# A macaron transformer layer on one core: the projection's stacked parts turned by f32r products with an identity, and one group's softmax maxima made in attention instead of the projection

## What is computed

```
x = x + 0.5 * ffn(layernorm(x))       # 8 experts of width 256, the 2 best of each row
x = x + attention(layernorm(x))       # 16 query heads, 4 key/value heads, head size 32
x = x + 0.5 * ffn(layernorm(x))

# attention
q, k, v = x @ wq, x @ wk, x @ wv      # 512, 128 and 128 columns
q, k = rope(q), rope(k)
p = softmax(causal(q k^T / sqrt(32)))
out = (p v) @ wo
```

## Time and profile before

| what | value |
|---|---|
| median of 3 runs | 1275.9 us (1274.03 to 1278.19) |
| the profiled execution's own time | 1275.88 us |
| its span in the trace | 1274.6 us |
| busy: PE, DVE, ACT, POOL | 93%, 71%, 52%, 47% of the span |
| projection, from the first product to the last copy | 273.5 to some 413.6 us |
| attention, first score to the last four | 413.96 to 1002.31 us |

### The profile page before, as it was taken

One profiled execution on the slowest core, in us unless ns is written; L12 is line 12 of the kernel. 1 busy time (PEld: TensorE's weight loads), 2 busy tenths in 40 slices (PEclk: granted clock), 3 DMA queues, 4 the chain that ended last, 5 costly groups with the idle time before them and its releaser, 6 DMA issues.

```text
span 1274.6 us, 20931 instructions
## 1 busy us (share of the span) xinstructions
PE 1179.8 (93%) x6837; PEld 757.3 (59%) x6837; DVE 910.2 (71%) x2132; ACT 659.6 (52%) x1305; POOL 600.5 (47%) x496
## 2 busy tenths in 40 slices
PE   4899999989998999999999999999999879999996
PEld 3678888758776544444545455445443346777774
DVE  8767777779997776576678787688755675666664
ACT  2545555536455554355456566356567744444442
POOL 4945444313210111001437556556582554888886
PEclk9899999999999999999999999999999999999999
DMA  9923333556530032013445845556633453666665
GB/s 335 367 96 108 111 109 108 174 168 120 96 63 4 34 70 35 1 53 83 99 101 159 173 100 125 174 133 173 135 93 66 139 204 66 100 102 102 101 105 73
DMA packets 68552, 148.44 MB, mean 116 GB/s; under 512 B 8832, under 2 KB 29312, under 8 KB 64448
## 3 DMA queue, kind: packets, MB, share of 16 engines
q0 software_dynamic: 35184, 93.34, 34.4%
q1 hardware_dynamic: 33264, 53.77, 12.4%
HBM read 81.28 MB, written 33.55 MB: 90 GB/s over the span
## 4 chain that ended last, share of the span: by engine, by line
PE 55%; DVE 19%; DMA 9%; issue 8%; POOL 6%; ACT 4%; SPq 0%; DVEq 0%; ACTq 0%; POOLq 0%
PE bank L839 10%; PE bank L1633 8%; PE bank L1645 8%; PE bank L997 7%; PE bank L862 5%; PE bank L1680 5%; DVE PM L1010 4%; PE bank L1663 3%; DVE bank L1012 3%; DMA out<-Y,DI 3%; POOL out L789 3%; DMA CD<-P 2%; DMA XG<-xn,TK 2%; PE bank L821 2%; PE bank L1395 2%
## 5 line engine op out<-in xcount | busy, mean ns | idle before, releaser
L1728 ACT ACTIVATE P<-bank 128x512 f32<-128x512 f32 (+3 forms) x640 | 304.6, 534 | 253.9 <-PE bank L1633 244.4
L1010 DVE TENSOR_REDUCE PM<-bank 128x1 f32<-128x512 f32 x384 | 252.4, 683 | 66.1 <-PE bank L997 65.7
L997 PE MATMUL bank<-Ks,Qs 96*128 96x512 f32 (+3 forms) x640 | 234.9, 387 | 15.1 <-DVE PM L1012 7.8
L1633 PE MATMUL bank<-Qs,Ks 98*128 98x512 f32 (+3 forms) x640 | 241.9, 408 | 5.7 <-ACT P L1728 3.4
L1633 PEld LDWEIGHTS bank<-Qs,Ks 98*128 98x128 f32 x640 | 116.6, 189 | 141.4 <-ACT P L1728 73.5
L1784 POOL TENSOR_SCALAR_AFFINE_SELECT P<-P 128x512 f32<-128x512 f32 x64 | 44.2, 702 | 277.3 <-ACT P L1728 228.8
L997 PEld LDWEIGHTS bank<-Ks,Qs 96*128 96x128 f32 x640 | 121.3, 190 | 64.3 <-DVE PM L1010 22.7
L1645 PE MATMUL bank<-P,V 128*32 128x512 f32 (+3 forms) x1280 | 152.0, 547 | 4.3 <-POOL P L1784 4.3
L1012 DVE CUSTOM_DVE_ANT_0 bank<-bank,KB 128x128 f32<-128x128 f32 (+3 forms) x256 | 124.1, 495 | 40.2 <-PE bank L997 39.6
L789 POOL DMA_INDIRECT out<-Y,DI x78 | 128.1, 1643 | 38.5 <-issue 32.6
L1798 POOL TENSOR_TENSOR CH<-CH,P 128x512 f32<-128x512 f32 x108 | 139.4, 1442 | 14.0 <-ACT P L1728 13.4
(11 more groups left out here) (193 smaller groups left out, 1935.9 us busy)
## 6 DMA issues: line engine op xcount, KB each, us to landing
CD<-P POOLq DMA_DIRECT2D x17, 1024.0 KB, 7.3
xn<-XN SPq DMA_DIRECT2D x8, 1024.0 KB, 7.9
WR<-L_ffn_w POOLq DMA_DIRECT2D x16, 512.0 KB, 15.6
XO<-y POOLq DMA_DIRECT2D x8, 1024.0 KB, 9.4
WR<-L_ffn_w SPq DMA_DIRECT2D x16, 512.0 KB, 7.8
CD<-P SPq DMA_DIRECT2D x7, 1024.0 KB, 5.3
CD<-CH POOLq DMA_DIRECT2D x7, 1024.0 KB, 6.8
XA<-y POOLq DMA_DIRECT2D x24, 256.0 KB, 4.2
```

Source lines behind the costliest of these rows:

```text
L997: pe.matmul(bk(g, bank)[:, 0:n], g.Qs[b][0:96, G % 4 * 4 + h, c * P:c * P + P], g.Ks[0:96, G % 4, k * BQ:k * BQ + n], start=True, stop=Tru ...
L1010: dve.tensor_reduce(dst, bk(g, bank)[:, 0:n], AX.X, ALU.max).then_inc(s(f"free{bank}"), 1)
L1633: pe.matmul(bk(g, bank)[:, o:BQ], g.Ks[0:98, G % 4, k * P:k * P + P], g.Qs[G // 4][0:98, G % 4 * 4 + j, o:BQ], start=True, stop=True).then ...
L1728: act.activation(a.P4[buffer_of(n)][:, j, o:BQ], bk(g, score_bank(g, i))[:, o:BQ], ACT.Exp, scale=scale).then_inc(s("exp"), 1)
```

## The change

Three edits. First, `stack` makes its 20 pieces with ordinary f32r products: `p.N` is the stationary operand as before and a copy of the identity in f32r, `p.IR`, the moving one. ACT makes that copy once at the start of the projection. Before, they were f32 transposes. Second, with EARLY = 3 only groups 0 to 2 have their tops in the projection (48, five in each odd tile from 5, six in each even one, the last four in tile 13, none in 14 and 15); group 3's 16 tops and its solvemax open attention's list. Third, the factor of the spread in attention is 1.13 in place of 1.1.

```diff
@@ memory
+    p.IR = t("IR", [P, P], F32R)
@@ project_plan
-    ahead = [key for G in range(4) for key in tops_of(G)]
+    ahead = [key for G in range(EARLY) for key in tops_of(G)]
...
-                if (total - done) % (total // 8) == 0 and done > total // 4 and i > 4 and ahead:
+                if (total - done) % (total // 8) == 0 and done > total // 4 + total // 8 * (i % 2) and i > 4 and ahead:
...
-        if told < (64 - len(ahead)) // 16:
+        if told < (16 * EARLY - len(ahead)) // 16:
@@ act_project
+    act.copy(p.IR[:], g.ident)
@@ pe_project, stack
-                ins = pe.transpose(bk(g, bank)[0:96, h * P:h * P + P], Nf[:, 4 * q + h, :], ident)
+                ins = pe.matmul(bk(g, bank)[0:96, h * P:h * P + P], p.N[:, 4 * q + h, :], p.IR[:], start=True, stop=True)
@@ attend_plan
-    ahead = [key for G in range(4, 4 * NB) for key in tops_of(G)]
+    ahead = [key for G in range(EARLY, 4 * NB) for key in tops_of(G)]
...
-            while ahead and given < 1.1 * weight:
+            while ahead and given < 1.13 * weight:
```

More of the change, by code:

```diff
@@ L19 @@
 KT = 4 * NB
+EARLY = 3
 F32 = mybir.dt.float32
@@ L1128, in project_plan @@
             told += 1
-    assert told == 4
-    g.shared = [("found", G) for G in range(4)]
+    assert told == EARLY
+    g.shared = [("found", G) for G in range(EARLY)]
 def turned_from_n(g, i):
@@ L1359, in pe_project @@
     s, pe, p, ident = g.s, g.nc.tensor, g.p, g.ident
-    Nf = p.N[:].bitcast(F32)
     def transp(i):
@@ L1507, in attend_plan @@
     ring, plan = g.ring, []
-    ahead = [key for G in range(4, 4 * NB) for key in tops_of(G)]
+    ahead = [key for G in range(EARLY, 4 * NB) for key in tops_of(G)]
     later = {}
-    told, weight, given, extra, known, solved, turned, free = 4, 0.0, 0.0, [], [], [], [], True
+    told, weight, given, extra, known, solved, turned, free = EARLY, 0.0, 0.0, [], [], [], [], True
     def put(at, step):
@@ L1526, in attend_plan @@
             weight += (BQ - first(b, k)) / BQ
-            while ahead and given < 1.1 * weight:
+            while ahead and given < 1.13 * weight:
                 key = ahead.pop(0)
+                assert key[1] < EARLY + 2 or ("solvemax", key[1] - 2) in plan, key
                 given += 1 if key[4] < key[1] // 4 else (key[3] + 1) / 4
```

## The result

The changed kernel takes **1285.89 us** (median of 6 runs, 1282.98 to 1287.06) against 1276.11 us (6 runs, 1273.06 to 1278.19): ratio 1.0066, 95% interval 1.0048 to 1.0083. It is slower by 9.8 us, outside the range given, and on the other side of no change. The profiled execution took 1287.06 us with a span of 1285.8.

What follows compares the result with a forecast made beforehand. With DVE bounding the projection and PE attention, -5.7 us in the projection and +4.4 us in attention summed to -1.3, from 1275.9 to 1274.6 us; the range for 8 in 10 was 1271.0 to 1278.4.

Steps and rivals of the forecast that it cites:

- What bounds each stage: DVE sets the pace in the projection and PE in attention; the change moves 16 tops across that border.
- The projection's -5.7 us: Sum of the projection's terms: fewer tops, faster stacks and a shorter way to the first score save 5.7 us.
- The stack's terms: Projection: f32r turning shortens a stack to some 2.1 us, 0.2 less; -0.5 before tile 5, -0.2 and -0.2 later.
- The price of a product: In the stack, one f32r product of a turned piece holds PE for 0.09 us, against 0.115 per transpose.
- the banks hold it: ACT empties the stack's banks at some 0.48 us apiece, so it takes some 2.1 us, though PE could do 1.8.
- The tiles without tops: Projection, tiles 14 and 15, PE-bound: without tops -1.0 and -0.6 us, each tile at 5.2 us.
- Attention's +4.4 us: Sum in attention: 2.4 for 16 tops, 0.5 for group 3's turn, 0.7 first weighed tile, 0.8 late maxima.
- The first weighed tile: Start of attention: fourteen tops before it in place of ten, 5.35 us after the first score, not 4.67; +0.7 us.
- late maxima: Attention: groups 8 and 4 turn later, so scores wait 0.5 and 0.3 us for their maxima; +0.8 us.
- the factor only spreads them: Attention: the factor 1.13 merely spreads the tops and was given no cost or gain.
- the route of the maxima is slow: Rival: first transfers at groups 4 and 8 take 4.1 us more each; one gives 1278.7, both 1282.8; chance 0.09.
- the clock: Attention: PE at granted 0.50 in single 3.4 us stretches, up to 1.7 us lost each; part of the range, no chance given.

Runs made afterwards that it cites:

- e5_busy_late: e4_late_sum with PE kept busy by 15 and 6 unused bf16 products on both sides of the last stack: 1274.86 us, ratio 0.9977.
- e10_busy_late_transposes: e5_busy_late with the f32 transposes put back in place of the f32r products: 1274.84 us, ratio 0.9989.
- e1_turn_only: The kernel before with the first edit alone, f32r products in place of f32 transposes: 1278.47 us, ratio 1.0007.
- e6_before_busy: The kernel before with 12 and 6 unused products keeping PE busy around the last stack: 1275.16 us, ratio 0.9984.
- e9_before_busy_factor: e6_before_busy with the factor 1.13, f32 transposes and all 64 tops in the projection: 1271.45 us, ratio 0.9957.
- e7_factor: The kernel before with the third edit alone, factor 1.13 in place of 1.1: 1275.91 us, ratio 0.9989.
- e4_late_sum: The changed kernel with block 1's 1 MB accumulating transfer put 12 scores later: 1279.17 us, ratio 1.0021.
- e11_factor_12: The changed kernel with 15 and 6 unused products around the last stack and factor 1.2, the 1 MB transfer unmoved: 1289.63 us, ratio 1.0103.
- e3_kept_busy: The changed kernel with 12 unused bf16 products on PE ahead of the last stack: 1283.81 us, ratio 1.0057.

## Why the prediction was wrong

**What bounds each stage** was read rightly: tops are DVE's in the projection and PE's in attention.

**The projection's -5.7 us.** It measured 4.0 in the changed kernel and 4.9 with the clock held (130.1 in e5_busy_late, 135.0 before). The stack's terms are the ones that were too large. The price of a product was right: twelve take 1.24 us, less one's own 0.25 over eleven steps 0.09 each, 0.09 forecast. That the banks hold it was right as well, but at more than 2.1 us. The changed kernel's third stack on PE, in order of time:

```profile
299.43 0.60 PE L1371 MATMUL bank<-K,XA 128*128 128x128 f32 x4
299.79 1.24 PE L1414 MATMUL bank<-IR,NA 128*96 128x128 f32 x12
301.19 1.04 PE L1414 MATMUL bank<-IR,NA 128*96 128x128 f32 x8 [0.16 <-ACT Qs L1327]
302.06 1.61 PE L1397 MATMUL bank<-WQH,XHA 128*128 128x512 f32 x8
```

The stack takes 302.06 - 299.79 = 2.27 us, where the same stack with transposes takes 2.20 (before and e10_busy_late_transposes) and the one in rows 4 took 2.29: no gain on PE. The fourth part has to wait for ACT's first copy and starts 1.40 us after the first one; five copies of 0.48 are 2.4 us of ACT's time however fast PE is. Of the 0.9 us put down to the turning (0.5, 0.2 and 0.2) 0.3 came (e10_busy_late_transposes), and none in e1_turn_only, 135.1 us from the first rotation to the first score against 135.0. The tiles without tops were right: 5.16 us of products in tile 14 (388.22 to 393.38), 5.02 in tile 15 (396.02 to 401.04), 5.2 forecast. The 0.9 us between 4.9 and 4.0 is the clock, below.

**Attention's +4.4 us** is right as a sum where nothing else disturbs: e5_busy_late 590.18 against e6_before_busy 585.74, 4.44. The parts are off against each other. The first weighed tile is 1.3 us later and not 0.7; the late maxima cost 0.4 at group 8; group 3 grew by 2.4 us, since group 4's turn moved into it out of group 2, and groups 1 and 2 gave 1.9 back. That the sum came out as forecast is in part luck: terms that were too small and gains that nobody forecast cancel. The balance with both disturbances taken away is -0.3 us (1274.86 and 1275.16), -1.3 forecast: a null. It compares a factor of 1.13 with one of 1.1. At the same factor the move seems to cost some 3 us (e10_busy_late_transposes against e9_before_busy_factor), so "the factor only spreads them", put at nothing, may hide a small gain; e7_factor alone did not show it.

**The step that failed is the term "late maxima" (+0.8 us)**, and with it the rival "the route of the maxima is slow", to which I gave 0.09. The term let group 8's first transfer take the 1.47 us of before and put the wait at 0.5; the transfer took 5.13 and the wait 4.18. I looked for traffic near group 4's turn only. At group 8 the 1 MB transfer was in the trace before, on POOL's queue at 602.89, behind the maxima that had left at 596.46; the turn's new place, eight scores later, puts the same 16 KB behind it. The wait was what the rival said, 4.1 us; its consequence was not priced: after 4 us without work PE ran at half clock for 13.7 us in this profile. Together they cost 8.2 us in the profiles, shown by e4_late_sum, and 5.7 to 6.7 by ratios and medians; e11_factor_12, which moves the turn ahead of the transfer, has no such wait either.

**The second failed step is "the clock"**: I counted on single stretches of 3.4 us, up to 1.7 us each, "part of the range". The changed kernel's fall lasted 17 us. It costs 3.8 us in group 0 and 0.9 before it (e4_late_sum against e5_busy_late; 4.3 us in the medians and 5.6 by the ratios, on two chips). Filling shows that it is the clock. What in the change makes the fall long is argued only: the move takes group 3's turn and tops away from where they stood around the last stack, and PE's pause there grew from 2.67 to 3.29 us, but e3_kept_busy with a pause of 0.69 fell as well, and e7_factor fell with 2.67. And it is not the change's alone: a like filling gives the kernel before 2.0 to 2.8 us.

The two make 8.2 + 4.7 = 12.9 of the 14.2 us between the spans of the changed kernel and e5_busy_late (1285.8 and 1271.6), 11.0 in the medians (1285.89 - 1274.86). By the ratios the slowdown of 0.66% divides so: 0.45% for the late maxima, 0.44% for the clock at attention's start less the 0.16% that the kernel before loses there as well, and -0.07% for all the rest. Each of these is uncertain by some 0.2%.

## What to carry to other kernels

A product whose output must be emptied by another engine is priced by the emptying: at 0.48 us a bank it hardly mattered whether PE took 0.09 or 0.11 us a piece. When a small latency-bound transfer is moved later in the program, look at every queue for what it now stands behind, not at the slack alone. And where work is taken away beside a pause of PE, price the clock, and give the kernel before the same filling before the loss is put down to the change: here 4.2 us without work cost up to 4 us more behind it, and keeping PE busy around the last stack was worth 4.7 us in the changed kernel and 2 to 3 in the one before.

## What the runs showed of the hardware

Most falls of the granted clock to 0.50 in attention, over all profiles here, lasted 3.4 us; in the changed kernel two lasted 13.7 and 17.1 us, with PE busy for 3.4 of 3.4 us in the last stretches of both. A wait of 4 us at group 8 was followed by 13.7 us at half clock in the changed kernel and by 3.4 us in e3_kept_busy. The Trainium skill, "TensorE: Matmul & The Clock Gate", section "What's actually happening", says that "the default state is throttled, and activity releases the throttle". At these two places the release came late: PE had been at work without a pause from 411.03 to 422.5 and from 614.44 to 627.2. What raised the clock there in the end no run here tells.

A transfer of 16 KB from SP took 1.45 to 1.5 us without other traffic and 5.13 us behind one of 1 MB whose issue on POOL had ended 1.1 us before its start.

The f32r product of 128 rows, 96 stationary and 128 moving columns takes 0.09 us in a row of such, the f32 transpose of the same piece 0.109 to 0.115. The product's weight load is a row of 0.159 to 0.165 us on PE's load queue, which overlaps the products.
